# A three-stage decoder layer on one core: GpSimd writes routed rows and results in another order

## The chip, the cores and the metric

The kernel runs on one core of a Trainium2 chip. The metric is the device time of one execution in microseconds (us). A core has TensorE (matmuls; its weight loads are shown apart), VectorE, ScalarE, GpSimd and SyncE, which here only issues transfers; sixteen DMA engines move the data.

## The reference

Each of 32 batches of 128 tokens with 128 features goes through three residual stages: self attention that keeps the 32 largest scores of a row, cross attention with 16 heads of 8 features over a context, and a feed-forward layer that sends every token to one of 8 experts. Only the last stage matters here:

```python
aff = feats @ centroids.T
eid = jnp.argmax(aff, axis=1)
...
for e in range(E):
    mask = (eid == e).astype(feats.dtype)[:, None]
    h = xhat * gamma[e] + beta[e]
    y = feats + jax.nn.relu(h @ w1[e] + b1[e]) @ w2[e] + b2[e]
    alpha = jax.nn.sigmoid(feats @ centroids[e])[:, None]
    out = out + mask * (alpha * y + (1.0 - alpha) * feats)
```

## The kernel before, in words

The 32 batches go through attention in 8 groups of four (`NG = 8`, `G = 4`). When a group's features are known, each token gets a row of a table in HBM, `routed_rows`, in which the tokens of an expert stand together. A token's payload in that table is 260 floats: the normed features, the residual, the gate alpha and the token's own number. `scatter_rows(f, j)` writes the 128 payloads of batch `j` of group `f` with one indirect DMA of GpSimd (130 KB); it waits for the group's slots, alpha and payload.

The feed-forward stage then runs over 39 tiles of 128 table rows (`NTILE = 39`). SyncE loads tile `t` into slot `t % 16` of a ring (`RING = 16`), and loads and results are counted in pairs: tiles 2m and 2m+1 share one semaphore. The first 16 tiles (`EARLY = 16`) hold rows of groups 0 to 5 only and are loaded before the last two groups are routed. Tile 16 waits for all payloads, for blank rows at each expert's end (eight stores of SyncE) and for the table of late tiles, which VectorE makes between tiles 6 and 10. Tile `t` from 16 on also waits until the results of both tiles of the pair that had its slots are written, since GpSimd reads the token numbers from the ring.

Per tile, TensorE transposes the rows (line 430), multiplies by the first weights (439) and, for the tile two before, by the second (452). ScalarE copies the transposed rows (502), scales the next expert's weights (510) and applies the relu (516). VectorE adds the first bias (475), the second (484) and makes the result (490). GpSimd scatters the result to `out` (528), again one indirect DMA. Below, T(n) is the start of tile n's transpose. In TensorE's program T(n) is followed by the first product of tile n-1 and the second of tile n-3. VectorE's queue runs alike, so that result n stands behind the second product that TensorE runs after T(n+3).

Every engine works through its own list in order, and semaphores alone tie them. The order in GpSimd's list around the change is written by hand: `ffn_pool` calls `last_group_part(t)` ahead of the result of tile `t`, and in it the remaining payloads are placed. Of the last two groups, 6 and 7, the payloads are written inside the feed-forward stage. `slots(f)` works out the rows of a group from counts that TensorE made and VectorE copied (line 1065).

Of the kernel before, what the change touches and what calls it, by code (L numbers as in the profile page):

```python
# [6 lines left out]
def preln_decoder_kernel(nc, T, out):  # L7
# [9 lines left out]

    B, S, D = T["x"].shape
    E, _, F = T["w1"].shape
    H, HD = 16, 8  # L20
    G = 4
    NG = B // G
# [7 lines left out]
    NTILE = B * S // 128 + E - 1  # L30
# [15 lines left out]
    with ExitStack() as stack:  # L46
# [6 lines left out]
        def sem(name):  # L53
            return stack.enter_context(nc.semaphore(name))
# [154 lines left out]
        s = {n: sem(n) for n in names}  # L209
# [11 lines left out]
        def wait_alone(eng, semaphore, n):  # L221

            eng.wait_ge(semaphore, n)
            if not isinstance(n, int):
                eng.nop(nofuse=True)

        def at(t, start, n, p=128):
            return t[0:p, ds(start, n)]

        def grouped(ap):  # L230
            return ap.rearrange("p (g n) -> p g n", g=G)

        def spread(ap, shape):
            return ap.to_broadcast(shape)
# [15 lines left out]
        def half(g):  # L250

            return g % 2
# [13 lines left out]
        def pay_of(f):  # L266

            return pay[:, half(f) * G:(half(f) + 1) * G, :]
# [12 lines left out]
        def later(g, first):  # L281

            return not isinstance(g, int) or g >= first
# [122 lines left out]
        def tiles(eng, step, first, last):  # L406
            for t in range(first, last):
                step(t // RING, t % RING)
# [86 lines left out]
        def ffn_scalar(act, last_group_part):  # L495
# [24 lines left out]
            act.wait_ge(s["ffn_loaded"], N_FFN)  # L520
            tiles(act, step, -2, NTILE)

        def ffn_pool(pool, last_group_part):
            for t in range(NTILE):
                last_group_part(t)
                k = t % RING
                pool.wait_ge(s["result_ready"], t + 1)
                pool.indirect_dma_start(out=out_rows,  # L528
                                        out_offset=bass.IndirectOffsetOnAxis(ap=ffn_row[k][:, TOKEN:TOKEN + 1].bitcast(U32), axis=0),
                                        in_=ffn_out[k], in_offset=None, bounds_check=B * S - 1,  # L530
                                        oob_is_err=False).then_inc(row_scattered[k // 2], 16)
            for pair in range(RING // 2):
                n = len([t for t in range(NTILE) if t % RING // 2 == pair])
                wait_alone(pool, row_scattered[pair], 16 * n)
# [180 lines left out]
        def slots(eng, f):  # L715

            wait_alone(eng, s["counts_read"], f + 1)
            wait_alone(eng, s["next_row_ready"], f + 1)
            eng.tensor_tensor(placed[:, :, :], counts[:, 0:G, :], spread(row(next_row[:, :]), [128, G, E]), ALU.add)\
               .then_inc(s["placed_step"], 1)  # L720
            wait_alone(eng, s["placed_step"], 5 * f + 1)
            if f < NG - 1:
                eng.tensor_tensor(next_row[:, :], next_row[:, :], counts[:, G, :], ALU.add).then_inc(s["next_row_ready"], 1)
            eng.tensor_tensor(placed[:, :, :], placed[:, :, :], onehot[:, 0:G, :], ALU.mult).then_inc(s["placed_step"], 1)
            for i, n in enumerate((E // 2, E // 4, E // 8)):
                wait_alone(eng, s["placed_step"], 5 * f + 2 + i)
                eng.tensor_tensor(placed[:, :, 0:n], placed[:, :, 0:n], placed[:, :, n:2 * n], ALU.add).then_inc(s["placed_step"], 1)
            if later(f, 2):
                wait_alone(eng, pay_stored[half(f)], 16 * G * (f // 2))
            wait_alone(eng, s["placed_step"], 5 * f + 5)  # L730
            eng.tensor_copy(slot[:, half(f) * G:(half(f) + 1) * G], placed[:, :, 0]).then_inc(s["slots_ready"], 1)
# [37 lines left out]
        def _(pool):  # L769
# [46 lines left out]
            def scatter_rows(f, j):  # L816

                if j == 0:
                    wait_alone(pool, s["pay_ready"], f + 1)
                    wait_alone(pool, s["tokens_ready"], f + 1)  # L820
                    wait_alone(pool, s["alpha_ready"], f + 1)
                    wait_alone(pool, s["slots_ready"], f + 1)
                at0 = half(f) * G + j
                pool.indirect_dma_start(out=rows, out_offset=bass.IndirectOffsetOnAxis(ap=slot[:, at0:at0 + 1].bitcast(U32), axis=0),  # L824
                                        in_=pay[:, at0, :], in_offset=None, bounds_check=E * CAP - 1,
                                        oob_is_err=False).then_inc(pay_stored[half(f)], 16)
# [62 lines left out]
            def second_rstd(f):  # L889

                wait_alone(pool, s["ln2_rstd"], f + 1)
                pool.tensor_tensor(var2[:, :], rstd[2][:, :], rstd[2][:, :], ALU.mult).then_inc(s["rstd2_step"], 1)
                wait_alone(pool, s["rstd2_step"], 3 * f + 1)
                pool.tensor_tensor(rstd2[:, :], var2[:, :], moments[2][:, half(f) * G:(half(f) + 1) * G, 1], ALU.mult)\
                    .then_inc(s["rstd2_step"], 1)
                wait_alone(pool, s["rstd2_step"], 3 * f + 2)
                pool.tensor_scalar(var2[:, :], rstd2[:, :], 1.0, EPS, ALU.mult, ALU.add).then_inc(s["rstd2_step"], 1)
                wait_alone(pool, s["rstd2_step"], 3 * f + 3)
                pool.tensor_tensor(rstd2[:, :], var2[:, :], minus_half[:, :], ALU.pow).then_inc(s["rstd2_ready"], 1)

            def sums_of_rows(f):

                second_rstd(f)
                if later(f, 2):
                    wait_alone(pool, pay_stored[half(f)], 16 * G * (f // 2))
                wait_alone(pool, s["feats_ready"], G * (f + 1))
                pool.tensor_tensor(pay_of(f)[:, :, D:2 * D], grouped(at(x2, half(f) * GS, GS)), grouped(feats[:, :]),
                                   ALU.add).then_inc(s["base_ready"], 1)
# [9 lines left out]

            def last_group_part(t):

                if 0 <= t < G:
                    scatter_rows(NG - 2, t)
                if t == 4:
                    slots(pool, NG - 1)
                if 0 <= t - 5 < G:
                    scatter_rows(NG - 1, t - 5)


            pool.memset(q_masked[:, MASKED:2 * MASKED], 0.0).then_inc(s["q_zeros_made"], 1)
# [17 lines left out]
            add_attended(NG - 1, 3)  # L947
            norm_rstd(pool, 2, NG - 1)
            slots(pool, NG - 2)
            sums_of_rows(NG - 1)  # L950
            normed_rows(NG - 1)
            ffn_pool(pool, last_group_part)


# [954 lines left out]
```

## Time and profile before

| | us |
|---|---|
| median of 3 runs | 393.71 |
| lowest, highest | 393.03, 395.42 |
| profiled execution, its own time | 394.67 |
| its span, first to last instruction | 392.9 |
| TensorE busy | 349.2 |
| VectorE busy | 295.1 |
| ScalarE busy | 240.8 |
| GpSimd busy | 199.0 |

Busy time is a sum over the whole span; it doesn't tell where an engine waited. The stretch from 287 us to the end is the feed-forward stage, and its timeline has to be read tile by tile. A timeline row gives the start, the duration, the engine, the line, what is written and read, and in square brackets the idle time ahead of it with what ended it; "remote" there means that no instruction of the trace was found that would have ended the wait just then, and "issue" that nothing was waited for.

### The profile page before, as it was taken

How to read it: one execution, taken by the hardware profiler on the slowest of the kernel's cores; microseconds unless marked ns; L12 is line 12 of the kernel's file. 1: busy time of each engine (PE TensorE's matmuls, PEld its weight loads, DVE VectorE, ACT ScalarE, POOL GpSimd, SP SyncE). 2: the span in 40 equal slices, each digit the busy share in tenths (PEclk: the TensorE clock that was granted, in tenths of full speed). 3: DMA queues.
4: the chain of work that ended last, by engine and by line, in shares of the span. 5: the costliest groups of instructions: out<-in, count | busy, mean ns of one | idle time of the engine just before them, and what ended most of it. 6: DMA issues, size and time to landing. Idle time of an engine off the chain costs nothing. (4 is left out here: it accounts for less than half of the span.)

```text
span 392.9 us, 11365 instructions
## 1 busy us (share of the span) xinstructions
PE 349.2 (89%) x3499; PEld 246.2 (63%) x3499; DVE 295.1 (75%) x1204; ACT 240.8 (61%) x527; POOL 199.0 (51%) x361
## 2 busy tenths in 40 slices
PE   5987989999999999999998999898989378999990
PEld 4766645655655655754664554555579368999980
DVE  6789866897999899899798957667646255667660
ACT  1474447578687787786676774646356245887740
POOL 4687420320550475475374374744728664455551
PEclk9899989999999999999999999999769788999995
DMA  6515101231231222222211132010243332543110
GB/s 142 161 24 178 45 27 23 53 107 25 53 86 26 50 77 67 53 75 63 52 26 58 24 93 58 20 43 0 83 119 96 103 129 77 148 126 90 33 32 0
DMA packets 30155, 26.96 MB, mean 69 GB/s; under 512 B 5891, under 2 KB 25479, under 8 KB 30096
## 3 DMA queue, kind: packets, MB, share of 16 engines
q1 hardware_dynamic: 26016, 19.59, 19.1%
q0 software_dynamic: 2784, 6.37, 4.7%
q8 instruction: 29, 0.48, 0.5%
q10 hardware_dynamic: 1296, 0.28, 0.5%
q14 instruction: 30, 0.25, 0.2%
HBM read 14.73 MB, written 8.01 MB: 58 GB/s over the span
## 5 line engine op out<-in xcount | busy, mean ns | idle before, releaser
L1013 DVE TENSOR_REDUCE neg_hmax<-s_bank 128x4 f32<-128x512 f32 x128 | 81.9, 682 | 31.4 <-PE s_bank L1568 31.2
L1312 ACT ACTIVATE weights<-s_bank 128x512 f32<-128x512 f32 x128 | 69.6, 594 | 26.4 <-PE s_bank L1586 25.7
L1579 PE MATMUL s_bank<-q_room,k_room 32*128 32x512 f32 x256 | 80.1, 646 | 0.4 <-ACT weights L1312 0.2
L1568 PE MATMUL s_bank<-k_room,q_room 32*128 32x512 f32 x256 | 79.0, 642 | 0.2 <-DVE neg_hmax L1013 0.2
L813 POOL TENSOR_TENSOR x<-x_bv,attended 128x128 f32<-128x128 f32 x32 | 14.6, 455 | 66.4 <-DVE attended L1040 66.4
L475 DVE TENSOR_TENSOR q_room<-s_bank,b_cols 128x512 f32<-128x512 f32 x39 | 27.0, 691 | 24.2 <-PE s_bank L439 13.9
L439 PE MATMUL s_bank<-q_room,self_room 128*128 128x128 f32 x312 | 44.9, 291 | 0.0
L1610 PE MATMUL pvt_bank<-weights,xv 128*32 128x128 f32 x1024 | 42.8, 285 | 0.6 <-ACT hmax_t L1303 0.6
L439 PEld LDWEIGHTS s_bank<-q_room,self_room 128*128 128x128 f32 x312 | 41.3, 206 | 0.0
L824 POOL DMA_INDIRECT routed_rows<-pay,slot x32 | 33.0, 1031 | 12.4 <-issue 7.9
L510 ACT ACTIVATE self_room<-w,gamma_t 128x512 f32 x39 | 28.2, 722 | 13.4 <-PE s_bank L439 9.0
L1579 PEld LDWEIGHTS s_bank<-q_room,k_room 32*128 32x128 f32 x256 | 25.2, 184 | 16.8 <-issue 10.1
L1610 PEld LDWEIGHTS pvt_bank<-weights,xv 128*32 128x32 f32 x1024 | 25.2, 111 | 15.8 <-ACT weights L1312 7.7
L1005 DVE MATCH_REPLACE8 self_room<-best,self_room 128x128 f32<-128x128 f32 x128 | 33.8, 275 | 0.0
L735 POOL TENSOR_SCALAR var_eps<-moments 128x4 f32<-128x4 f32 x24 | 4.8, 201 | 54.6 <-DVE moments L695 54.1
L516 ACT ACTIVATE q_room<-q_room 128x512 f32<-128x512 f32 x39 | 24.6, 630 | 12.3 <-DVE q_room L475 6.1
L528 POOL DMA_INDIRECT out<-x_in,k_room x23 | 22.5, 978 | 18.2 <-DVE x_in L490 10.5
L1586 PEld LDWEIGHTS s_bank<-hmax_t,head_sel 32*128 32x128 bf16 x512 | 20.3, 93 | 16.9 <-issue 13.7
L1586 PE MATMUL s_bank<-hmax_t,head_sel 32*128 32x128 bf16 x512 | 29.7, 217 | 0.0
L1303 ACT ACTIVATE hmax_t<-pvt_bank 128x128 bf16<-128x128 bf16 x32 | 8.9, 278 | 30.7 <-PE pvt_bank L1596 29.5
L999 DVE MAX8 best<-self_room 128x8 f32<-128x128 f32 x128 | 27.6, 277 | 0.1
L740 POOL TENSOR_TENSOR rstd<-var_eps,minus_half 128x4 f32<-128x4 f32 x24 | 24.6, 1027 | 3.7 <-POOL var_eps L735 0.6
(214 smaller groups left out, 746.9 us busy)
## 6 DMA issues: line engine op xcount, KB each, us to landing
w<-in_w SPq DMA_DIRECT2D x16, 256.0 KB, 4.1
k_room<-routed_rows SPq DMA_DIRECT2D x31, 130.0 KB
x_in<-in_x SPq DMA_DIRECT2D x8, 256.0 KB, 3.4
ctx_in<-in_ctx SPq DMA_DIRECT2D x8, 256.0 KB, 2.9
k_room<-k_room SPq DMA_DIRECT2D x128, 16.0 KB
q_room<-q_room SPq DMA_DIRECT2D x112, 16.0 KB
routed_rows<-blank SPq DMA_DIRECT2D x9, 130.0 KB
q_room<-routed_rows SPq DMA_DIRECT2D x8, 130.0 KB
```

The costliest lines, as they stand in the source:

```text
L439: m = pe.matmul(s1_bank[:, (k % 2) * F + c * 128:(k % 2) * F + (c + 1) * 128], ffn_w1[k % 2][:, c * 128:(c + 1) * 128], ffn_row_t[k % 2], ...
L475: dve.tensor_tensor(by_chunk(ffn_hid[k % 2]), by_chunk(s1_bank[:, (k % 2) * F:(k % 2 + 1) * F]), spread(at(b1_cols, e * FC, FC).rearrange( ...
L510: act.activation(ffn_w1[k % 2], at(w1, e * F, F), ACT.Identity, scale=at(gamma_t, e, 1)).then_inc(s["w1_picked"], 1)
L824: pool.indirect_dma_start(out=rows, out_offset=bass.IndirectOffsetOnAxis(ap=slot[:, at0:at0 + 1].bitcast(U32), axis=0), in_=pay[:, at0, :] ...
L999: dve.max(best8[:, b, r, :], at(src, b * S, S)).then_inc(s["topk_step"], 1)
L1005: dve.match_replace(at(left, b * S, S), best8[:, b, r, :], at(src, b * S, S), TAKEN)\
L1013: dve.tensor_reduce(neg_hmax[:, first:first + 4], bank.rearrange("p (h k) -> p h k", k=S), AX.X, ALU.max, negate=True).then_inc(s["s1_max" ...
L1312: act.activation(weights[:, u, :], s2_bank[:, (u % 2) * GS:(u % 2 + 1) * GS], ACT.Exp, scale=HEAD_SCALE).then_inc(s["s2_exp"], 1)
L1568: pe.matmul(s1_bank[:, (u % 2) * GS:(u % 2 + 1) * GS], natural(q_nat, g, j, strip(u)), masked(k_masked, K_RING, g, j, strip(u)), start=Tru ...
L1579: pe.matmul(s2_bank[:, (u % 2) * GS:(u % 2 + 1) * GS], natural(k_nat, g, j, u), masked(q_masked, Q_RING, g, j, u), start=True, stop=False)
L1586: m = pe.matmul(s2_bank[:, (u % 2) * GS + i * S:(u % 2) * GS + (i + 1) * S], head_sel[32 * u:32 * (u + 1), i, :], hmax_t[32 * u:32 * (u + ...
L1610: m = pe.matmul(pvt_bank[32 * i:32 * (i + 1), (u % 2) * S:(u % 2 + 1) * S], xv[:, block:block + 32], weights[:, u, i * S:(i + 1) * S], sta ...
```

## The change

The order in GpSimd's list changes and the count of results that it waits for; no other engine's list does. The four payload scatters of group 6 move ahead of the last group's sums. Those of group 7 stand in one row ahead of the result of tile 2. The result of tile t from 2 on waits until up to eight further results are made; this number is 8 for tiles 2 to 9, then falls by one at tiles 10, 13, 17, 20, 24, 27, 31 and 34, to 0.

```diff
+        def results_before(t):
+
+            behind = 10 * (NTILE - 2 - t) // (NTILE - 4) if t >= 2 else 0
+            return min(NTILE, t + 1 + max(0, min(behind, 8)))
+
         def ffn_pool(pool, last_group_part):
             for t in range(NTILE):
                 last_group_part(t)
                 k = t % RING
-                pool.wait_ge(s["result_ready"], t + 1)
+                pool.wait_ge(s["result_ready"], results_before(t))
...
             def last_group_part(t):
 
-                if 0 <= t < G:
-                    scatter_rows(NG - 2, t)
-                if t == 4:
+                if t == 2:
                     slots(pool, NG - 1)
-                if 0 <= t - 5 < G:
-                    scatter_rows(NG - 1, t - 5)
+                    for j in range(G):
+                        scatter_rows(NG - 1, j)
...
             slots(pool, NG - 2)
+            for j in range(G):
+                scatter_rows(NG - 2, j)
             sums_of_rows(NG - 1)
             normed_rows(NG - 1)
             ffn_pool(pool, last_group_part)
```

GpSimd's list before, from the end of group 6's slots to the result of tile 1 (`pay` and `slot` are the payloads and their rows, `x_in` holds results):

```order
L731 CAST slot<-placed 128x4
L892 TENSOR_TENSOR var<-rstd 128x4
L894 TENSOR_TENSOR rstd<-var,moments 128x4
L897 TENSOR_SCALAR var<-rstd 128x4
L899 TENSOR_TENSOR rstd<-var,minus_half 128x4
L907 TENSOR_TENSOR pay<-x,feats 128x4x128
L913 TENSOR_TENSOR pay<-feats,rstd 128x4x128
L916 IOTA pay 128x4
L824 DMA routed_rows<-pay,slot 33920x260
L528 DMA out<-x_in,k_room 4096x128
```

The same place now (lines of the changed file stand five further down):

```order
L736 CAST slot<-placed 128x4
L829 DMA routed_rows<-pay,slot 33920x260 x4
L897 TENSOR_TENSOR var<-rstd 128x4
L899 TENSOR_TENSOR rstd<-var,moments 128x4
L902 TENSOR_SCALAR var<-rstd 128x4
L904 TENSOR_TENSOR rstd<-var,minus_half 128x4
L912 TENSOR_TENSOR pay<-x,feats 128x4x128
L918 TENSOR_TENSOR pay<-feats,rstd 128x4x128
L921 IOTA pay 128x4
L533 DMA out<-x_in,k_room 4096x128 x2
```

All four payload scatters of group 6 stand ahead of the seven instructions of group 7 that they stood behind, and results 0 and 1 follow each other.

GpSimd's list before, from the fourth result (tile 3) to the seventh payload of the stage:

```order
L528 DMA out<-x_in,k_room 4096x128
L719 TENSOR_TENSOR placed<-counts,next_row 128x32
L724 TENSOR_TENSOR placed<-placed,onehot 128x32
L727 TENSOR_TENSOR placed<-placed 128x4x4
L727 TENSOR_TENSOR placed<-placed 128x4x2
L727 TENSOR_TENSOR placed<-placed 128x4
L731 CAST slot<-placed 128x4
L528 DMA out<-x_in,k_room 4096x128
L824 DMA routed_rows<-pay,slot 33920x260
L528 DMA out<-x_in,k_room 4096x128
L824 DMA routed_rows<-pay,slot 33920x260
```

And now, from the slots of group 7, which follow the result of tile 1:

```order
L724 TENSOR_TENSOR placed<-counts,next_row 128x32
L729 TENSOR_TENSOR placed<-placed,onehot 128x32
L732 TENSOR_TENSOR placed<-placed 128x4x4
L732 TENSOR_TENSOR placed<-placed 128x4x2
L732 TENSOR_TENSOR placed<-placed 128x4
L736 CAST slot<-placed 128x4
L829 DMA routed_rows<-pay,slot 33920x260 x4
L533 DMA out<-x_in,k_room 4096x128 x6
L533 DMA out<-q_room,k_room 4096x128 x4
```

Group 7's slots and payloads stand ahead of the results of tiles 2 to 7, no longer between those of tiles 3 to 8.

## Rows read from the trace of the kernel before

**Rows 1.** Windows, two stretches: busy time by engine (instructions), granted clock, DMA share, GB/s
```profile
304.50:334.60 30.10, 19.32 (x137) 18.71 (x138) 13.81 (x45) 12.80 (x25) 17.53 (x23) 0.83 0.32 103
334.60:376.30 41.70, 41.70 (x377) 41.70 (x376) 29.00 (x67) 33.36 (x67) 21.53 (x23) 1.00 0.35 95
```

**Rows 2.** Timeline of TensorE: transposes of tiles 8, 9, 10, 12, 15, 16, 38
```profile
304.45 0.30 PE L430 MATMUL s_bank<-ident,k_room 128*128 128x128 f32 x1 [0.26 <-ACT q_room L502]
313.24 0.45 PE L430 MATMUL s_bank<-ident,k_room 128*128 128x128 f32 x1 [6.58 <-ACT q_room L502]
316.78 0.27 PE L430 MATMUL s_bank<-ident,k_room 128*128 128x128 f32 x1
...
323.76 0.45 PE L430 MATMUL s_bank<-ident,q_room 128*128 128x128 f32 x1 [2.83 <-ACT q_room L502]
...
332.50 0.30 PE L430 MATMUL s_bank<-ident,q_room 128*128 128x128 f32 x1 [1.38 <-ACT q_room L502]
334.59 0.27 PE L430 MATMUL s_bank<-ident,k_room 128*128 128x128 f32 x1
...
376.30 0.27 PE L430 MATMUL s_bank<-ident,k_room 128*128 128x128 f32 x1
```

**Rows 3.** Timelines: tile 4's second product, then ScalarE and VectorE behind the gap
```profile
303.04 1.15 PE L452 MATMUL pvt_bank<-w,q_room 128*128 x8
...
312.82 0.28 ACT L502 ACTIVATE q_room<-s_bank 128x128 f32<-128x128 f32 x1 [5.75 <-remote]
...
312.89 0.29 DVE L484 TENSOR_TENSOR q_room<-pvt_bank,x_in 128x128 f32<-128x128 f32 x1 [5.82 <-remote]
```

**Rows 4.** Timeline of GpSimd: first and last of eight scatters in a row, last payload
```profile
301.26 1.09 POOL L824 DMA_INDIRECT routed_rows<-pay,slot  x1 [0.17 <-issue]
...
310.31 0.97 POOL L528 DMA_INDIRECT out<-x_in,k_room  x1 [0.30 <-issue]
...
326.16 0.98 POOL L824 DMA_INDIRECT routed_rows<-pay,slot  x1 [0.30 <-issue]
```

**Rows 5.** Timelines around group 5's four payloads: GpSimd, TensorE, VectorE
```profile
274.29 1.08 POOL L824 DMA_INDIRECT routed_rows<-pay,slot  x1 [0.90 <-POOL slot L731]
...
278.23 0.97 POOL L824 DMA_INDIRECT routed_rows<-pay,slot  x1 [0.30 <-issue]
...
276.91 1.03 PE L1730 MATMUL att_bank<-cent_t,feats_t 128*128 128x8 f32 x8 [0.19 <-issue]
...
276.18 0.26 DVE L1035 RECIPROCAL wsum_inv<-att_bank 128x16 f32<-128x16 f32 x1 [1.86 <-PE att_bank L1624]
...
280.22 0.19 DVE L1134 COPY aff<-att_bank 128x32 f32<-128x32 f32 x1 [1.79 <-remote]
```

**Rows 6.** Timelines: first and last step of group 6's slots; VectorE's copy of counts
```profile
294.85 0.25 POOL L719 TENSOR_TENSOR placed<-counts,next_row 128x32 f32<-128x32 f32 x1 [3.43 <-DVE counts L1065]
...
296.73 0.19 POOL L731 CAST slot<-placed 128x4 int32<-128x4 f32 x1
...
306.33 0.19 DVE L1065 COPY counts<-att_bank 128x40 f32<-128x40 f32 x1
```

**Rows 7.** Windows on the granted clock where TensorE stood still from 320.92
```profile
323.20:323.60 0.40, 0.00 (x0) 0.00 (x0) 0.19 (x1) 0.26 (x1) 0.00 (x0) 0.82 0.01 0
```

**Rows 8.** Timelines: results 13 and 19 scattered; load of tile 35
```profile
338.27 0.98 POOL L528 DMA_INDIRECT out<-q_room  x1 [0.90 <-issue]
...
349.84 0.98 POOL L528 DMA_INDIRECT out<-x_in,k_room  x1 [1.12 <-DVE x_in L490]
...
354.15 0.34 SPq L547 DMA_DIRECT2D k_room<-routed_rows  x1
```

**Rows 9.** DMA engines' busy tenths, 40 slices of 353.5 to 357.2; page: us to landing
```profile
DMA  0000064298973100977964998100000000000100
...
wv<-in_wv SPq DMA_DIRECT2D x1, 64.0 KB, 2.6
```

**Rows 10.** Timeline of GpSimd: the last scatter
```profile
384.32 0.98 POOL L528 DMA_INDIRECT out<-x_in,k_room  x1 [0.30 <-issue]
```

## The prediction, made before the changed kernel had run

> **What bounds the kernel now.** The change touches only GpSimd's list from 296.9 us on, so I read the feed-forward stage alone: windows for its two halves first, then TensorE's timeline for the pace of the tiles, then the other engines at each gap.
>
> From T(16) to T(38) TensorE is busy all of the 41.70 us at full clock [rows 1]. T(16) is 334.59 and T(38) 376.30 [rows 2]: 41.71 / 22 = 1.896 us a tile. GpSimd, with half a stretch busy, has slack there. In the half before, TensorE is busy 19.32 of 30.10 us at clock 0.83 [rows 1]. T(8) to T(16) takes 334.59 - 304.45 = 30.14 us where eight tiles at that pace take 15.17: 15.0 us are lost. They lie in a few places [rows 2]: tile 9 comes 8.79 us after tile 8 (6.9 lost), tile 10 another 3.54 after it (1.6 lost, at half clock), tile 12 follows an idle of 2.83, tile 15 one of 1.38.
>
> What ends these gaps matters most. VectorE takes up tile 4's second product at 312.89, after 5.82 idle and marked "remote", though TensorE had run it by 303.04 + 1.15 = 304.19; ScalarE comes back at the same moment [rows 3]. No data was missing. What ran meanwhile is GpSimd: eight indirect DMAs 1.28 us apart from 301.26 to 311.28 [rows 4]. TensorE's signals came through about 1.5 us after the last. The same shows on a smaller scale at group 5's payloads, four in a row from 274.29 to 279.20: a product of TensorE that ended by 276.18 was read at once, one that ended at 276.91 + 1.03 = 277.94 only at 280.22, which is 1.0 us after the row's end [rows 5]. I call this a hold: while indirect DMAs with payloads among them run 0.30 us apart, TensorE's signals to other engines queue up. It begins 1.9 to 3.6 us after the row's start. From T(16) on, with one scatter in every 1.9 us, there is none. The first hold, 304.19 to 312.8, is 8.6 us long and cost 6.9, or 80%; the rest is work already queued.
>
> The trace shows the holds, not their mechanism. On DMAs it shows nothing that is full in them (share 0.32 [rows 1]).
>
> **The change: payloads in two rows.** Group 6's four start 0.90 after its slots, as group 5's did [rows 5]: 296.92 + 0.90 = 297.8 [rows 6], and last 279.20 - 274.29 = 4.9, to 302.7. Alpha and payload of group 6 are older than that, so they don't wait. Hold A then runs to 303.8 and begins at 299.7 to 301.4: 2.4 to 4.1 us long. I take the early beginning, since it is nearer to the first signal that the row of eight caught, 304.19 - 301.26 = 2.9 us in. What is queued behind them on GpSimd, group 7's sums and normed rows, moves by 4.9 us; only group 7's own payloads wait for it. Before, it ended at 301.1 [rows 4]; now it does at 307. Results 0 and 1 take 307.2 to 309.5, with nobody waiting (tiles 16 and 17 need them). The slots of group 7 need counts that VectorE copies at 306.33 [rows 6]; even 1 us later they are there. Slots take 296.92 - 294.85 = 2.1 and the pause 0.9, so the second row runs from 312.5 to 317.4, hold B from 314.4 at the earliest to 318.5. The last payload leaves 9.7 us earlier than the 326.16 + 0.98 of before [rows 4]; so nothing of the table holds tile 16 back, which was close to it before.
>
> Losses of each hold: 80% of 4.1 is 3.3, of the short form 2.4 it is 1.9. Behind B add 1.6 for the half clock, as behind the first hold before; behind A, where TensorE would stand still for some 2.2 us, none. T(16) would then be 304.45 + 15.17 + 3.3 + 3.3 + 1.6 = 327.8. With both short and no half clock it is 323.4; with the half clock twice and a further 1.6 for the stretch that VectorE spends on the late tiles' table, 331. **Term 1: 327.8 - 334.59 = -6.8 us** (bounds -11.2 and -3.6).
>
> **The change: results up to eight tiles late.** This adds a wait, and SyncE stands behind it: tiles 18 and 19 are loaded when results 2 and 3 are written, and result 3 now waits for result 11. In the steady part result 13's scatter starts at 338.27, which is T(16) + 3.68 [rows 2, 8]. So scatter 3 starts at T(14) + 3.68. From the start of the pair's second scatter to the pair's second load it takes 354.15 - 349.84 = 4.31 [rows 8]. That load's packets are through in slice 26 of 40, at 355.9, 1.75 after the issue; a smaller load of the page took 2.6 to its landing [rows 9]. I take 2.1, nearer the load itself. Together T(18) can't be before T(14) + 10.1, where the pace gives T(14) + 7.6: TensorE waits 2.5 us (bounds 2.2 and 3.0). The next pair, 20 and 21, hangs on T(16) in the same way and is just met, since T(18) has been pushed. Pair 22 and 23 hangs on T(18): 2.5 again. Tile 26 hangs on result 18 (seven late): T(21) + 10.1, no wait behind the others. From tile 28 on, six late or fewer, there is slack. **Term 2: 2 x 2.5 = +5.0 us** (bounds +4.4 and +6.0, and nothing if the row path is shorter than the rows say).
>
> The Trainium skill, "DMA: Bandwidth & Descriptors", section "Rules for kernel authors", advises to issue a DMA early and to wait on its semaphore late, which speaks against holding finished results back at all. By the rows only the eight- and seven-late ones cost anything; by the rule alone one would look for a cost at every late result, and the sum would be slower than mine.
>
> Does the clock fall in these waits? It stayed full after an idle of 1.38; after the idle from 320.92 it fell only inside 323.20 to 323.60 [rows 7], 2.3 to 2.7 us in. With 2.5 of idle it is at the edge. I take no fall; with one at each, 2 x 1.6 = +3.2.
>
> Where the lateness falls by one, two results leave together, 1.28 apart, eight times. Before, results leave 0.30 apart without a payload among them only at the end [rows 10], with nobody behind them. I take them as free; the bound is the hold of a short row.
>
> **The end.** Results 33 and 34 leave together, so 34 starts 1.28 late; the slack in front of the last ones takes up all but 0.2 of it. The last scatter at 384.32 and the 8 us behind it stay as they are. **Term 3: +0.2.** Nothing is added or removed on other engines.
>
> **Sum.** -6.8 + 5.0 + 0.2 = -1.6 us. The profiled execution took 394.67 with a span of 392.9 and lies 0.96 above the median; on it the sum gives 393.1, on the median of 393.71 it gives **392.1**.
>
> **Rivals.**
>
> Short holds, row wait as reckoned: -11.2 + 5.0 + 0.2 = -6.0, 387.7. For it: in the row at 274 signals passed for 1.9 us and perhaps for 3.6. Against: in the row of eight one was caught 2.9 us in.
>
> Short or long holds, but no wait for rows: -6.8 + 0.2 = 387.1, or -11.0 = 382.7 at best. It needs the path from scatter to loaded row to be under 7.6 - 3.7 = 3.9 us instead of 6.4, which no row supports.
>
> Slower: the pairs of results make holds of their own. The place is tiles 14 to 38, where TensorE has no slack. A pair lasts 2.3 us and the signals would come 1.0 after it; a hold that begins 1.9 in is 1.4 long, at 80% 1.1, and eight of them make 8.8. Then -1.6 + 8.8 = +7.2, 400.9. It becomes slower than before from 0.2 us a pair on. For it: in the row of eight, half were results. Against: GpSimd can't run further than a pair, since it waits for results that TensorE must first make, and every hold that the trace shows has a payload in its row.
>
> The clock falls at both waits for rows: -1.6 + 3.2 = +1.6, 395.3.
>
> The change doesn't do what it says: the gaps aren't caused by GpSimd's rows but, say, by instructions that arrive late. Then term 1 is gone and 5.2 remain: 398.9. Against it: two engines that had different lists came back 0.07 us apart, and just after GpSimd's row. The Trainium skill, "Runtime: NRT & Kernel Launch", section "Instruction fetch mechanics", says that the sequencer streams its code ahead and that this is mostly hidden unless a branch is taken; the list here is unrolled.
>
> **How the numbers follow.** A measurement of this kernel can tell about 1%, 3.9 us, from no change: faster is below 389.8, slower above 397.6. Forecast (389.8 to 394) 0.41; clock at both waits 0.13; short holds 0.20; no wait for rows 0.07; pairs with holds 0.14; gaps from elsewhere 0.05. Faster: 0.20 + 0.07 and a sliver of the forecast, 0.28. Slower: 0.14 + 0.05, 0.19. Same: 0.53. The range leaves out the best cases below 386.5 (0.08) and the worse half of the slow ones above 399 (0.1).
>
> **What would show it.** In the profile after: GpSimd's payloads near 298 to 303 and 312 to 317; no gap of 5.8 "remote" on VectorE; T(16) near 328; TensorE idle about 2.5 us ahead of T(18) and T(22), with full DMA queues behind a scatter that waited for a result eight tiles on; then 1.9 us a tile to the end. The prediction is wrong if T(16) comes after 331 (holds are longer than rows of four showed), if T(18) and T(22) come without a wait, or if TensorE shows gaps again behind tile 26.

## Result and the profile after

The changed kernel took 405.06 us (median of 4 runs, 404.13 to 405.93), the kernel before 394.56 beside it (4 runs): ratio 1.0278, 95% interval 1.0235 to 1.0322. Ratios, here and in the table below, are taken over the fast runs of both kernels and aren't the quotient of the two medians, from which they differ by up to 0.5%. The profiled execution took 405.57 with a span of 403.8, against 392.9 before. The forecast was 392.1, and its range ended at 399.0.

T(n) is again the start of tile n's transpose. The stretch from T(16) to T(38), in which TensorE had no slack before [rows 1], now reads as follows (windows; columns as in [rows 1]):

```profile
core 0 of [0], span 403.8 us
326.54:383.17 56.63, 46.25 (x377) 44.26 (x375) 28.32 (x67) 33.61 (x67) 27.68 (x29) 0.97 0.29 79
```

TensorE is busy 46.25 of 56.63 us for work that took 41.71. In order: T(16) comes at 326.54, 8.05 us earlier than before [rows 2]. T(0), which the change doesn't touch, came 1.23 us later in this run (288.65, before 287.42), so from T(0) on the gain is 9.28. Then 14.92 us are lost up to T(38), and 4.00 more from T(38) to the start of the last scatter (12.02 us against 8.02; it starts at 395.19, before at 384.32 [rows 2, 10]). The sum is +10.87, the whole difference of the spans.

Two kinds of idle time make the loss. Four rows of the list of waits from 326 us on (us in total, times, longest):

```profile
ACT q_room L502 <- remote: 8.1, 6, 1.6
PE s_bank L430 <- ACT q_room L502: 5.4, 6, 1.2
DVE q_room L484 <- remote: 5.1, 3, 1.9
PE s_bank L430 <- DMA k_room<-routed_rows: 4.7, 3, 2.5
```

The last row is the wait for input rows that hang on late results. TensorE's timeline has it at T(18), T(22) and T(24):

```profile
333.00 0.33 PE L430 MATMUL s_bank<-ident,k_room 128*128 128x128 f32 x1 [2.50 <-DMA k_room<-routed_rows]
335.83 0.42 PE L430 MATMUL s_bank<-ident,k_room 128*128 128x128 f32 x1
...
343.91 0.33 PE L430 MATMUL s_bank<-ident,k_room 128*128 128x128 f32 x1 [1.47 <-DMA k_room<-routed_rows]
...
348.62 0.33 PE L430 MATMUL s_bank<-ident,k_room 128*128 128x128 f32 x1 [0.69 <-DMA k_room<-routed_rows]
```

The first is the 2.5 us of the forecast. Behind it TensorE ran at a granted clock of 0.60 for 3 us (window 335 to 338), and T(19) comes 2.83 after T(18) and T(20) another 2.65 after it, instead of 1.90 each. T(24) comes 22.08 us after T(16), where eight tiles at the pace take 15.17: 6.9 us are lost up to it. No wait in this stretch is marked remote. The other 8.0 are lost between T(24) and T(38).

Two other rows of the list are marked "remote", the mark that the holds of before had [rows 3]; in the second of the four TensorE waits for ScalarE, mostly behind such places. One such place, lines picked out of all engines (so are those of the timelines further down):

```profile
348.13 0.98 POOL L533 DMA_INDIRECT out<-q_room  x1 [2.43 <-DVE x_in L490]
349.41 0.97 POOL L533 DMA_INDIRECT out<-q_room  x1 [0.30 <-DVE x_in L490]
349.68 1.06 PE L452 MATMUL self_bank<-w,q_room 128*128 x8
350.69 0.98 POOL L533 DMA_INDIRECT out<-q_room  x1 [0.30 <-issue]
352.53 0.28 ACT L502 ACTIVATE q_room<-s_bank 128x128 f32<-128x128 f32 x1 [1.18 <-remote]
352.60 0.29 DVE L484 TENSOR_TENSOR q_room<-self_bank,x_in 128x128 f32<-128x128 f32 x1 [1.92 <-remote]
352.95 0.30 PE L430 MATMUL s_bank<-ident,k_room 128*128 128x128 f32 x1 [0.31 <-ACT q_room L502]
```

The product that VectorE needs ended at 350.74, and VectorE takes it up 1.86 later, 0.93 after GpSimd's row has ended. It is a hold, and there is no payload in the row: three results, 1.28 us apart. Five such threes are written between T(24) and T(38), so each costs some 1.6 us. The prediction had reckoned with twos.

### The profile page after: what moved, and what is told of

The parts are those of the page before. It is cut to its first block and busy times, and to the rows that moved or that the text cites. A ratio compares the mean times of both kernels' runs of the same rounds, so it can differ in the third digit from the quotient of the medians.

```text
span 403.8 us, 11365 instructions
## 1 busy us (share of the span) xinstructions
PE 354.2 (88%) x3499; PEld 246.9 (61%) x3499; DVE 294.7 (73%) x1204; ACT 241.3 (60%) x527; POOL 199.0 (49%) x361
## 5 line engine op out<-in xcount | busy, mean ns | idle before, releaser
L439 PEld LDWEIGHTS s_bank<-q_room,self_room 128*128 128x128 f32 x312 | 40.0, 201 | 0.5 <-issue 0.5
```

The lines of the kernel that those rows point to most:

```text
L439: m = pe.matmul(s1_bank[:, (k % 2) * F + c * 128:(k % 2) * F + (c + 1) * 128], ffn_w1[k % 2][:, c * 128:(c + 1) * 128], ffn_row_t[k % 2], ...
```

## Experiments

Two theories stood first. **A**: three or more results in a row, 1.28 us apart, make holds, and these are the larger part. **B**: only the waits for input rows cost. A third came up with the first call. In the table are all runs: the chip by the number its result gives (the first comparison gives none), the time, the kernel before beside it, and from the trace, in us, T(0) to T(16), T(16) to T(38), and T(38) to the last scatter.

| run | chip | us | before | ratio (95%) | 0-16 | 16-38 | 38-end |
|---|---|---|---|---|---|---|---|
| before | - | 393.71 | | | 47.17 | 41.71 | 8.02 |
| after | - | 405.06 | 394.56 | 1.028 (1.024-1.032) | 37.89 | 56.63 | 12.02 |
| e1_payload_rows | 10 | 380.58 | 387.25 | 0.980 (0.974-0.986) | 36.63 | 41.71 | 8.03 |
| e2_late_from_9 | 10 | 392.14 | 387.25 | 1.011 (1.004-1.018) | 41.79 | 47.79 | 8.60 |
| e3_tokens_copied | 10 | 381.74 | 387.25 | 0.984 (0.978-0.990) | 36.91 | 41.71 | 8.39 |
| e4_groups | 10 | 393.57 | 387.25 | 1.012 (1.004-1.019) | 42.34 | 44.07 | 11.88 |
| before_again | 5 | 395.33 | 395.50 | one run | 46.31 | 41.77 | 8.03 |
| after_again | 5 | 406.72 | 395.50 | 1.028 (1.017-1.039) | 38.49 | 58.31 | 11.22 |
| e1_again | 5 | 394.65 | 395.50 | one run | 47.10 | 41.71 | 8.03 |
| e4_again | 5 | 402.53 | 395.50 | one run | 46.10 | 45.07 | 14.44 |
| e3_again | 5 | 401.50 | 394.61 | 1.018 (1.012-1.024) | 38.98 | 54.10 | 11.10 |
| e6_spaced_payloads | 5 | 404.08 | 394.61 | 1.023 (1.017-1.030) | 38.54 | 56.25 | 12.55 |
| e7_spaced_groups | 5 | 395.63 | 394.61 | one run | 46.01 | 41.80 | 13.08 |
| e2_again | 5 | 410.74 | 394.61 | one run | 46.70 | 55.49 | 9.72 |
| e8_pause_every_second | 0 | 386.14 | 386.85 | 0.998 (0.995-1.002) | 37.65 | 41.71 | 13.05 |
| e9_pause_short | 0 | 387.72 | 386.85 | 1.001 (0.997-1.006) | 37.89 | 41.71 | 12.57 |
| after_third | 0 | 388.77 | 386.85 | 1.003 (0.998-1.007) | 37.24 | 48.94 | 8.61 |
| e10_after_spaced | 11 | 399.26 | 393.34 | 1.014 (1.010-1.018) | 37.76 | 49.69 | 16.04 |
| e8b_pause_every_second | 11 | 393.96 | 393.34 | 0.997 (0.992-1.002) | 46.29 | 43.68 | 8.50 |
| e9b_pause_short | 11 | 394.60 | 393.34 | 0.999 (0.995-1.003) | 46.62 | 42.43 | 8.49 |

**First call, e1 to e4.** The payload rows alone; then the lateness alone on the kernel before; then the changed kernel without the wait for rows; then groups of a known size.

```diff
 e1, on the changed kernel
-                pool.wait_ge(s["result_ready"], results_before(t))
+                pool.wait_ge(s["result_ready"], t + 1)
 e2, on the kernel before: results_before as in the change, with
+            behind = 10 * (NTILE - 2 - t) // (NTILE - 4) if t >= 9 else 0
 e3, on the changed kernel: VectorE, behind each result
+                    dve.tensor_copy(tokens[:, k:k + 1], ffn_row[k][:, TOKEN:TOKEN + 1].bitcast(I32)).then_inc(s["result_ready"], 1)
 e3: the scatter's addresses; SyncE's load of a row
+                                        out_offset=bass.IndirectOffsetOnAxis(ap=tokens[:, k:k + 1].bitcast(U32), axis=0),
-                    rows_scattered(sp, t)
+                    wait_alone(sp, s["result_ready"], t - RING + 1)
 e4, on the kernel before
+            for first, end, n in ((17, 23, 2), (23, 29, 3), (29, 37, 4)):
+                if first <= t < end:
+                    return first + (t - first) // n * n + n
+            return t + 1
```

> The changed kernel with its payload rows kept and every result written on time, as before the change. Theory A (rows of GpSimd's indirect DMAs, results alone too, hold TensorE's signals up from the third in a row on): behind the second payload row GpSimd has eight or more finished results to write, 1.28 us apart, about 318.4 to 330. They make one long hold there, some 10 us at 80%, so T(16) moves from 326.5 back to about 334, and from there on it is 1.9 us a tile without a gap: 393 to 395 us. Theory B (only the waits of TensorE for its input rows cost, a row of results alone holds nothing): T(16) stays at 326.5, no wait behind it, last scatter near 376.5: 386 us.

> The kernel before the change, with the payloads where they were, and with the lateness of the changed kernel for tiles 9 to 36 alone. Both theories leave T(16) at 334.6. Theory B: the load of tiles 24 and 25 hangs on result 9, which waits for result 17; 2.5 us at T(24) and perhaps once more behind it, then 1.896 us a tile to T(38) and 8.0 us to the last scatter: 396 to 399 us. Theory A: the catch-up of the results, two and three at a time 1.28 us apart, costs 7.5 us between T(26) and T(38) and 4.0 behind T(38) as in the changed kernel, whatever the row waits add: 405 to 410 us, with VectorE and ScalarE idle 1 to 2 us, marked remote, behind every group of three.

> The changed kernel, but VectorE copies each result's column of token numbers into a small tile of its own as soon as the result is made, the scatter takes its addresses from that copy, and SyncE loads a row buffer again once VectorE has freed it, not when GpSimd has written the result sixteen tiles back. So a late result holds up no load. All else stands, the lateness and the pairs and threes of results too. Theory A (holds from threes of results are the larger part): the 4.7 us of waits for input rows and the clock stretch behind them go, the gaps marked remote and the 4.0 behind T(38) stay: 397 to 400 us. Theory B (the late input rows are the cause, and the rest follows from the tiles having fallen out of step): T(16) at 326.5, then 1.9 us a tile to 368.3 and 8 behind it: 385 to 388 us.

> The kernel before the change; results 17 to 22 leave two at a time, 23 to 28 three at a time, 29 to 36 four at a time, each group when its last result is made. No result is more than three late, so no input row is. Theory A: pairs cost nothing or up to 0.3 us each; a group of three ends in a hold that costs 1 to 1.5 us, one of four 2 to 3 us, since the row grows by 1.28 and the losses by 80% of that: 2 x 1.2 + 2 x 2.5 = 7.4 us on top, about 401 us, with T(16) at 334.6 and the pace at 1.9 us a tile up to T(24). Theory B: no hold behind results alone: within 1 us of before, 393 to 395 us.

The two theories could not be told apart in this call, because the kernel before itself took 387.25 instead of 394.56, and the holds had gone, those of the untouched part too. e2 has the payloads where the kernel before has them, in its row of eight. Its timeline around that row, and around T(16):

```profile
299.29 0.99 POOL L829 DMA_INDIRECT routed_rows<-pay,slot  x1 [0.30 <-issue]
...
300.59 0.97 POOL L533 DMA_INDIRECT out<-x_in,k_room  x1 [0.30 <-issue]
301.82 0.27 PE L430 MATMUL s_bank<-ident,k_room 128*128 128x128 f32 x1
301.86 0.97 POOL L829 DMA_INDIRECT routed_rows<-pay,slot  x1 [0.31 <-issue]
...
318.09 0.98 POOL L829 DMA_INDIRECT routed_rows<-pay,slot  x1 [0.30 <-issue]
...
325.21 0.48 PE L430 MATMUL s_bank<-ident,k_room 128*128 128x128 f32 x1 [6.45 <-DMA k_room<-routed_rows]
```

T(9), at 301.82, is 1.99 behind T(8); before it was 8.79 with the same row [rows 2, 4]. On this chip what sets T(16) is the last payload: it starts at 318.09, and tile 16's rows are there 7.1 later. That is why e1 gains 2% here: its last payload starts at 312.52. e2 and e4 are slower than before by 1.1 and 1.2%. In e2 6.1 us lie between T(16) and T(38), the waits for rows at T(24) and behind it and 3.5 us at a granted clock of 0.50 (window 325.5 to 329) behind T(16); in e4 3.8 lie at the end, where results 33 to 38 leave in one row from 376.49 on.

**Second call: the two kernels of the comparison again, unchanged, with e1 and e4.** No edit.

> The kernel before the change, word for word, with its trace. In the four runs ahead of this one it took 387.25 us where it had taken 394.56, and e2_late_from_9 and e4_groups, which keep its placement of the payloads, ran their row of eight without any gap marked remote. Theory C (whether GpSimd's rows hold TensorE's signals up depends on the chip that runs the kernel): either a run near 394 us with the gap of 8.8 behind T(8), or one near 387 us with T(9) 2.0 behind T(8) and a single wait of 6 to 7 us for the table's rows at T(16); nothing between. Theory D (the edits of the other kernels took the holds away by where they put instructions): 394 us with the holds in every case.

> The changed kernel, word for word. Theory C, if this call's kernel before runs near 387 us: no gap marked remote anywhere, T(16) near 320, two waits for input rows of 2.5 us at T(18) and T(22) with the clock falling at most once, then 1.9 us a tile: 320 + 41.7 + 5 + 1.6 + 16.6 to the end, 385 us and a ratio of 0.99 to 1.00. If the kernel before runs near 394 us: 405 us as before, ratio 1.028. Theory D: ratio 1.028 in either case.

> Payload rows alone again. Where signals are held up: a long hold from 318 to 332 behind the second payload row, T(16) near 334 and 393 to 395 us. Where not: 380 to 382 us with T(16) near 320.6 as in the first run of it.

> Results 17 to 36 in twos, threes and fours on the kernel before, again. Where signals are held up: gaps marked remote behind every group of three and four, 7 us in all on top of the kernel before. Where not: T(26) to T(38) at 1.9 us a tile, as in the first run of it, and the time of the kernel before plus the 5 to 7 us that the run showed.

The call got another chip, and everything was back: 395.3, 406.7 and a ratio of 1.028 again. Theory C held, D fell. Each call had one chip, so what differs might also be something else about the call; chip 5 alone was had twice, with holds both times. e1_again shows A's long hold behind the second payload row, which nothing but plain results prolongs:

```profile
316.52 0.98 POOL L829 DMA_INDIRECT routed_rows<-pay,slot  x1 [0.30 <-issue]
317.80 0.98 POOL L533 DMA_INDIRECT out<-x_in,k_room  x1 [0.30 <-issue]
...
324.21 0.98 POOL L533 DMA_INDIRECT out<-x_in,k_room  x1 [0.30 <-issue]
327.11 0.28 ACT L502 ACTIVATE q_room<-s_bank 128x128 f32<-128x128 f32 x1 [7.22 <-remote]
327.18 0.29 DVE L484 TENSOR_TENSOR q_room<-pvt_bank,x_in 128x128 f32<-128x128 f32 x1 [7.12 <-remote]
```

Here the results follow the payloads until 325.2, and both engines come back 1.9 us later, after more than 7 us. The whole gain of the payload rows is gone (T(0) to T(16) 47.10; before_again, on the same chip, 46.31). B had expected no effect of a row of results. e4_again doses it. Results in twos leave the pace at 1.90 us a tile from T(17) to T(25); T(26) to T(38) takes 25.95 instead of 22.75. Two rows of three lie in that stretch, from 360.29 and from 367.29; the first four starts only at 376.01, 1.7 us ahead of T(38). Here is one of the twos:

```profile
345.90 0.98 POOL L535 DMA_INDIRECT out<-x_in,k_room  x1 [2.81 <-DVE x_in L490]
346.02 0.27 PE L430 MATMUL s_bank<-ident,k_room 128*128 128x128 f32 x1
347.18 0.98 POOL L535 DMA_INDIRECT out<-x_in,k_room  x1 [0.30 <-issue]
347.91 0.27 PE L430 MATMUL s_bank<-ident,k_room 128*128 128x128 f32 x1
```

So the prediction's "I take them as free" is all but right for a two that stands alone: the tiles behind the twos come at 1.90 to 2.05 us.

**Third call.** e3 and e2 again, e6 (e3 with pauses between payloads) and e7 (e4 with pauses inside its groups). The pause is a memset of 0.55 us on a tile of its own; with it two indirect DMAs start 1.69 us apart.

```diff
+        def short_pause(pool):
+            if pauses:
+                pool.wait_ge(s["paused"], len(pauses))
+            pauses.append(0)
+            pool.memset(pause[:, :], 0.0).then_inc(s["paused"], 1)
 e6, in scatter_rows
+                if j > 0:
+                    short_pause(pool)
 e7, ahead of the scatter's wait
+                if t >= 17 and results_before(t) == results_before(t - 1):
+                    short_pause(pool)
```

> The changed kernel with the tokens copied, so that no input row waits for a late result, on whatever chip this call gets. If its kernel before runs near 387 us (no holds on that chip): 381 to 382 us as in the first run. If near 395 us: theory A (threes of results make holds by themselves): T(16) near 326, the 4.7 us of waits for rows gone, but 5 us or more of gaps marked remote between T(16) and T(38) and 4 more behind it, 397 to 400 us. Theory A2 (results leave in threes only because the waits for rows have put the tiles out of step; on time they leave in twos, and twos are free as e4_again showed): 1.9 us a tile from T(16) on, no remote gap, 386 to 388 us.

> The same kernel with the tokens copied, and a memset of half a microsecond on GpSimd between the payloads of each row of four, so that they start 1.8 us apart and not 1.28. If holds come from the spacing of 0.30 us between one indirect DMA and the next: the gap of 1.9 us behind T(6) and the one behind T(12) vanish, T(16) comes 2 to 3 us earlier against T(0) than in e3_again, 384 to 386 us. If they come from the payloads as such: T(0) to T(16) as in e3_again. On a chip without holds: as e3_again, within 1 us.

> The kernel e4 (results 17 to 36 in twos, threes and fours) with the same memset between the results of a group. If spacing decides: T(24) to T(38) at 1.9 us a tile with no gap marked remote, where e4_again lost 3.3 us there, and some 2 us more off the end: 397 us. If the number in the row decides: as e4_again, 402 us, or worse, since rows last longer. On a chip without holds: 393 us, as e4_groups.

> Lateness of results 9 to 36 alone, on the kernel before. On a chip with holds: T(16) near 335, the wait for rows near T(24) worth 4.2 us as in the first run, and holds behind threes of results after it: 402 to 406 us. On one without: 392 us as in the first run.

e3_again decides between A and B: no tile waits for its rows, and T(16) to T(38) still takes 54.10. Its 401.5 us are 1.5 above what A had expected. It also shows why A2 fell. The first hold stands in a stretch in which all tiles were on time:

```profile
336.61 0.98 POOL L536 DMA_INDIRECT out<-q_room,tokens  x1 [0.92 <-issue]
337.90 0.98 POOL L536 DMA_INDIRECT out<-q_room,tokens  x1 [0.30 <-issue]
339.18 0.98 POOL L536 DMA_INDIRECT out<-q_room,tokens  x1 [0.30 <-issue]
341.08 0.28 ACT L504 ACTIVATE q_room<-s_bank 128x128 f32<-128x128 f32 x1 [0.91 <-remote]
341.51 0.30 PE L431 MATMUL s_bank<-ident,k_room 128*128 128x128 f32 x1 [0.89 <-ACT q_room L504]
```

The lateness falls by one, so the second leaves 1.28 behind the first. The third is due 1.90 behind the first, while the second still runs, and starts right behind it. **A catch-up by one is a row of three**, 3.55 us long. The hold (T(24) comes 2.95 after T(23)) delays the results of several tiles, which then arrive together: the next row on GpSimd, at 342.69, has four.

e7 settles the part of the spacing. It has the groups of e4, and this pace:

```profile
358.63 0.98 POOL L546 DMA_INDIRECT out<-q_room,k_room  x1 [0.17 <-issue]
358.95 0.27 PE L431 MATMUL s_bank<-ident,q_room 128*128 128x128 f32 x1
359.60 0.54 POOL L530 MEMSET pause<- 128x512 bf16 x1
360.31 0.98 POOL L546 DMA_INDIRECT out<-q_room,k_room  x1 [0.17 <-issue]
360.84 0.27 PE L431 MATMUL s_bank<-ident,k_room 128*128 128x128 f32 x1
```

T(24) to T(38) takes 26.54 us where e4_again took 29.84 and the kernel before 26.55: threes 1.69 us apart hold nothing. Behind its fours, which start at 370.43, no wait is marked remote either. In e6 the gap at T(7) goes too (2.03 us, e3_again 3.82), but the last payload then starts at 318.78, and tile 16 waits 2.7 us for its rows and starts a stretch at half clock. It gained 0.5 us up to T(16), where 2 to 3 were expected, and lost more behind it to rows like those of e3_again: 404.1 us, not the 384 to 386 of its expectation, which had left these rows out. e2_again at 410.7 is slower than the 402 to 406 expected, by holds between T(28) and T(38).

**Fourth and fifth call.** e8 and e9 (built on e6) were to write every result on time and only space them. As they ran they kept the changed kernel's lateness, since the wait on the copied tokens still counted it, and the chip had no holds, so they tell only that the slower catch-up costs 4.5 to 5 us at the end there. e8b and e9b are the two as meant, and e10 spaces the results of the changed kernel.

```diff
 e8b (e8 leaves results_before in the first wait)
+                pool.wait_ge(s["result_ready"], t + 1)
+                if t >= 2 and t % 2 == 0:
+                    short_pause(pool)
+                pool.wait_ge(s["result_made"], t + 1)
 e8b, in scatter_rows
+                if j == 2:
+                    short_pause(pool)
 e9b: a memset half as wide; "if t >= 2:" and "if j > 0:" in their place
 e10, on the changed kernel
+                if t > 2:
+                    short_pause(pool)
                 pool.wait_ge(s["result_ready"], results_before(t))
```

> Payload rows as in the changed kernel with one pause of half a microsecond in the middle of each, tokens copied, every result written as soon as it is made, and such a pause before every second result, so that a backlog leaves 1.28 and 1.69 us apart in turn. If it takes three in a row at 1.28 us to make a hold: no gap marked remote behind T(6) nor behind T(12), T(16) 37 to 38.5 us behind T(0), 1.9 us a tile to T(38), a backlog of two or three results at the end for some 2 us: 385 to 388 us on the chip with holds. If the mean spacing of 1.49 us is what counts and is too short: a long hold behind the second payload row as in e1_again, 393 to 396 us. On a chip without holds: 381 to 383 us.

> The same with a pause half as long before every payload but the first of a row and before every result from 2 on: 1.45 us apart throughout. If what counts is each single gap between two indirect DMAs and 0.47 us is enough: as e8, 385 to 388 us on the chip with holds. If not: holds behind both payload rows and a long one behind the backlog, 393 to 396 us. On a chip without holds: 381 to 383 us.

> The changed kernel, word for word, a third time. On a chip where its kernel before runs near 394 us: 403 to 407 us, ratio 1.02 to 1.03. On one where that runs near 387 us: no gap marked remote, waits of about 2.5 us for input rows at two places and once a stretch at half clock, 385 to 388 us, ratio 0.99 to 1.00.

> The changed kernel with the pause of half a microsecond on GpSimd before each result from the third on, so that no two start less than 1.69 us apart. Its waits for input rows stay. On a chip with holds: if the spacing is the cause, no gap marked remote behind T(16), T(16) to T(38) 41.7 + 5 for the rows + 2 to 4 at half clock, 49 to 51 us where the changed kernel took 56.6 and 58.3, and 2 to 3 us more at the end for the slower catch-up: 397 to 401 us. If not, T(16) to T(38) 55 us or more and 405 us. On a chip without holds: T(16) to T(38) as in after_third, 48.9 us, 388 to 391 us.

> As e8 was meant: payload rows with one pause in the middle of each, tokens copied, every result written as soon as it is made, a pause before every second one. On a chip with holds: if it takes three indirect DMAs in a row at 1.28 us to make a hold, no gap marked remote behind T(6), T(16) 37 to 38.5 us behind T(0), then 1.9 us a tile and a backlog of some results at the end: 385 to 388 us. If the mean spacing of 1.49 us is too short, a long hold behind the second payload row as in e1_again: 393 to 396 us. On a chip without holds: 381 to 383 us.

> As e9 was meant: the same with half the pause before every payload but the first of a row and before every result from 2 on, 1.45 us apart throughout. On a chip with holds: 385 to 388 us if that gap is enough, 393 to 396 us if not. On a chip without holds: 381 to 383 us.

after_third is the changed kernel with its holds taken away by the chip, e10 the same by spacing. Chip 11 is one with holds: e10's payload rows, left at 1.28 us, still have T(7) 3.78 after T(6), where after_third has 2.02. Both keep the waits for rows. The trace of e10 is of the slowest of its five runs, 402.4 us. First the windows from T(16) to T(38), of after_third and of e10:

```profile
320.80:369.74 48.94, 44.17 (x377) 43.56 (x376) 29.00 (x67) 33.54 (x67) 27.68 (x29) 0.97 0.33 92
```

```profile
325.92:375.61 49.69, 44.10 (x376) 43.34 (x375) 29.01 (x67) 33.78 (x67) 38.93 (x51) 0.97 0.30 87
```

48.94 and 49.69 us, against 56.63 and 58.31 with both. In either, TensorE waits 4.7 us for the same tiles' rows, and no wait behind T(16) is marked remote; in e10 0.8 come on top at T(28), because its slower catch-up keeps that result late too. From 348.77 to 356.47 after_third writes seven results in a row, with T(n) at 1.90 meanwhile. It has the two waits where the forecast put them, and a triple of results with no wait marked remote behind it:

```profile
327.16 0.40 PE L430 MATMUL s_bank<-ident,k_room 128*128 128x128 f32 x1 [2.41 <-DMA k_room<-routed_rows]
330.74 0.27 PE L430 MATMUL s_bank<-ident,k_room 128*128 128x128 f32 x1
...
336.32 0.97 POOL L533 DMA_INDIRECT out<-q_room,k_room  x1 [0.92 <-DVE x_in L490]
337.60 0.97 POOL L533 DMA_INDIRECT out<-q_room,k_room  x1 [0.30 <-DVE x_in L490]
338.87 0.33 PE L430 MATMUL s_bank<-ident,k_room 128*128 128x128 f32 x1 [2.28 <-DMA k_room<-routed_rows]
338.88 0.98 POOL L533 DMA_INDIRECT out<-q_room,k_room  x1 [0.30 <-issue]
```

e10's results start 1.69 us apart, thirteen in a row from 347.59 to 367.87 and on to the end, with T(n) at 1.90 from T(30) on. But a GpSimd that may write one in 1.69 us catches up slowly: 16.04 us from T(38) to the last scatter. e8b and e9b bound the spacing from the other side: 1.28 and 1.69 in turn, or 1.47 throughout, hold as soon as the row is long. The trace of e8b is of its slowest run (397.5 us, 3.5 above the median), so the reading rests on e9b (395.2). In e9b, in and behind a row of twelve from 312.11 to 329.37:

```profile
323.27 0.29 DVE L486 TENSOR_TENSOR q_room<-self_bank,x_in 128x128 f32<-128x128 f32 x1 [3.50 <-remote]
...
327.69 0.72 ACT L513 ACTIVATE self_room<-w,gamma_t 128x512 f32 x1 [4.22 <-remote]
```

T(16) is then 46.3 and 46.6 behind T(0), where the kernel before has 46.3 to 47.2, and both kernels are level with it.

## Why the prediction was wrong

**What bounds the kernel now: right.** GpSimd's rows are what held TensorE's signals: e6, e7 and e10 took holds away by spacing the indirect DMAs alone, with the lists of VectorE and ScalarE as they were, which instructions that arrive late don't explain. What the prediction took too narrowly is "with payloads among them".

**Term 1: right in sum, not in its parts.** T(16) moved by -8.05 where -6.8 was forecast, inside its bounds; from T(0) on it is -9.28, and -7.8 in after_again against before_again. The term held 8.2 us of losses: 3.3 for each of two holds and 1.6 for a half clock. In after, hold A made T(7) come 3.88 after T(6), 2.0 over the pace:

```profile
304.40 0.28 ACT L502 ACTIVATE q_room<-s_bank 128x128 f32<-128x128 f32 x1 [0.75 <-remote]
304.83 0.30 PE L430 MATMUL s_bank<-ident,k_room 128*128 128x128 f32 x1 [0.36 <-ACT q_room L502]
```

Behind the second payload row no wait is marked remote. T(13) comes 3.19 after T(12), 1.3 over the pace, and the granted clock is 1.00 all the way to T(16). The rest of what was lost is in steps of about 2.5 us between T(9) and T(14), a stretch in which VectorE also works on the late tiles' table; after_third, without holds, has them too. The forecast had them in its bound alone. That the errors nearly cancel is luck.

**Term 2: right in place, short in size.** The two waits came at T(18) and T(22), 2.57 and 2.43 us over the pace in after_third: 5.0, as forecast. Wrong was "I take no fall" of the clock. T(19) comes 3.58 behind T(18), 1.7 over the pace at full clock, after one of the two waits; the window 329 to 332 of after_third has a granted clock of 0.72. The length of the wait alone doesn't tell which: in after_third, after_again and e10 the clock fell behind the wait of 2.3 to 2.4 us ahead of T(18), and stayed full behind that of 2.25 to 2.4 ahead of T(22). With 0.5 more at T(23) to T(25) the lateness costs 7.2 us there; e10, without the 1.0 that T(28) comes late, gives 7.0, and after itself lost 6.9 up to T(24).

The Trainium skill's advice of "DMA: Bandwidth & Descriptors", section "Rules for kernel authors", to issue early, read as the prediction read it, would have charged every late result. after_third has row waits at T(18) and T(22) and none worth the name behind; e3_tokens_copied, as late but with its loads freed, runs at 1.9 us a tile from T(16) on. On a chip without holds lateness itself is all but free (0.4 us at the end); what hangs on it isn't.

**The step that failed** is "Where the lateness falls by one, two results leave together [...] I take them as free". The rival on the slower side had the mechanism, holds by results alone, and got 0.14. Its sum of +8.8 comes near what was lost by the wrong count, eight pairs at 1.1 each; there were five threes at 1.6 ahead of T(38). What the prediction set against that rival, that "GpSimd can't run further than a pair", missed the next result: it falls due 0.6 us after the second of the two has started, so each catch-up is a row of three. And "every hold that the trace shows has a payload in its row" was true of the trace, but no row without payloads had been there to look at ahead of T(38); e1_again and e4_again show that plain results hold as well. Its size, from after: of the 14.92 us lost between T(16) and T(38), 8.0 lie between T(24) and T(38), where all the waits marked remote are. Taking 7.0 to 7.2 off for the row waits, as e10 and after_third have them, leaves nearly the same, 7.7 to 7.9.

**Term 3** was +0.2, and +4.0 came. after_third has +0.6, so by subtraction about 3.4 is the same mechanism. The account is then -8.05 (up to T(16)), +6.9 (late rows), +8.0 (holds), +4.0 (end, 3.4 of it holds): +10.9. Taken one at a time these don't add up: with the row waits removed (e3_again) the holds alone lose 12.4 us there, so the two share some of their time; how they share it I didn't take apart.

**What the forecast couldn't know.** The four chips fall in two kinds. With holds (the first comparison, 5, 11) the kernel before takes 393 to 395.5 us, without (10, 0) 387. The change was timed on one kind twice (the first comparison and chip 5), 1.028 both times, and on the other once (chip 0), 1.003. The payload rows alone are 2% faster without holds (chip 10) and level with them, in a single run (chip 5). On chip 11 GpSimd's scatters last 0.98 us and follow after 0.30 like on chip 0, so its own list shows no difference. What does differ between the chips, or between the calls, isn't in the traces, and stays open.

None of the kernels beats before on both kinds. The payload rows with results on time (e1) come nearest: 0.980 on chip 10 and 394.65 beside 395.5 on chip 5.

## What to carry to other kernels

A list that lets work pile up and then catches up must be read for rows, not pairs: add the piece that falls due while the released ones still run. If something is made late on purpose, first cut what hangs on it; one small copy removed all waits for rows that hung on late results (e3_again). And time such a change on more than one chip: the same two kernels gave 1.028 and 1.003.

## What the runs showed of the hardware

On chips 5 and 11 indirect DMAs of GpSimd hold up TensorE's signals by their rate. A two 1.28 us apart costs 0.15 at most (e4_again, T(26) and T(27)). A three costs 1.2 to 1.9 us over the next three or four tiles (e4_again, e3_again), and a row of eight 7 us (before, e4_again). At 1.47 us apart a row of twelve still does it (e9b). At 1.69 apart neither four payloads (e6) nor more than a dozen results (e10) do. On chip 10 twenty-one in a row, 1.28 to 1.40 us apart (e1, 308.49 to 334.33), held nothing.

The signals don't wait for the end of the row. Inside before's row of eight, which ends at 311.28, VectorE takes up a product of TensorE that ended at 303.14, 2.6 us late:

```profile
302.05 1.09 PE L439 MATMUL s_bank<-q_room,self_room 128*128 128x128 f32 x8
305.72 0.69 DVE L475 TENSOR_TENSOR q_room<-s_bank,b_cols 128x512 f32<-128x512 f32 x1 [1.65 <-remote]
```

The next, ended at 304.19, comes 8.7 late [rows 3]. Lateness that grows along a row would fit a queue which takes between 1.5 and 1.7 us for each indirect DMA. That is an estimate from the spacings above, and isn't shown: no run looked into it.
